# Attention and feed-forward on eight cores: fills spread over whole tiles, square roots split in two steps, and an end worked in subtiles

## The reference

```python
def layernorm(x): return (x - mean(x)) / sqrt(var(x) + 1e-5)
# x: (4, 4096, 1024), 16 heads of 64
q, k, v = heads(ln(x) @ Wq + bq), heads(ln(x) @ Wk + bk), heads(ln(x) @ Wv + bv)
att = q @ k.T / 8
mask = tril(ones(T, T)) * (arange(T) % 4 != 3)      # causal, and every fourth key dropped
att = softmax(where(mask == 0, -inf, att))
x = x + ln((att @ v) @ Wp + bp)
idx = argmax(log_softmax(logits) + gumbel(u))       # one of 8 weight matrices
x = x + ln(ln(x) @ W[idx] + b[idx])
```

## Time and profile before

| | us |
|---|---|
| Median of 3 runs (lowest to highest) | 746.71 (746.45 to 749.49) |
| The profiled execution | 743.47 |
| Its span on the slowest core, core 6 | 741.9 |
| Spans of the eight cores | 733.8 to 741.9 |
| PE, ACT, DVE, POOL busy | 649.0, 530.2, 418.1, 144.0 |

### The profile page before, as it was taken

The page is one execution under the profiler, slowest core; times in us unless marked ns, Lnnn a source line. Parts: engine busy times, 40 slices in busy tenths (PEclk is TensorE's granted clock), DMA queues, the critical chain, the costliest instruction groups (busy, mean ns, idle before and its releaser), DMA issues.

```text
span 741.3 us, 24579 instructions; the slowest of 8 cores (733.8 to 741.9 us)
## 1 busy us (share of the span) xinstructions
PE 649.0 (88%) x9452; PEld 283.8 (38%) x9460; DVE 418.1 (56%) x744; ACT 530.2 (72%) x718; POOL 144.0 (19%) x238
## 2 busy tenths in 40 slices
PE   1788989889898999999999998889999999999846
PEld 1444435344344444333433433333333333333312
DVE  3327766765655463653333333277766776986484
ACT  3233356344698787888878888888898989888246
POOL 1010013122122112212111124110120110760104
PEclk9979999899999999999999999999999999999989
DMA  8989467955357062123400035602233223142224
GB/s 161 185 184 159 147 173 154 208 83 109 99 115 165 18 132 44 32 46 55 93 17 17 18 59 84 190 16 74 83 77 88 75 88 105 34 138 87 102 57 142
DMA packets 78240, 72.47 MB, mean 98 GB/s; under 512 B 58544, under 2 KB 58800, under 8 KB 78128
## 3 DMA queue, kind: packets, MB, share of 16 engines
q1 hardware_dynamic: 72060, 59.50, 31.9%
q0 software_dynamic: 5696, 11.14, 9.6%
q10 hardware_dynamic: 372, 0.27, 0.2%
HBM read 60.68 MB, written 8.52 MB: 93 GB/s over the span
## 4 chain that ended last, share of the span: by engine, by line
PE 50%; ACT 15%; issue 15%; DMA 11%; DVE 6%; SPq 1%; ACTq 1%; POOL 1%; DVEq 0%; POOLq 0%
PE pj L673 23%; ACT Pr L1223 12%; PE sps L744 10%; PE yz L781 7%; PE yz L799 4%; DMA wkb<-wk 3%; DMA wvb<-wv 2%; PE yz L671 2%; DMA fmQ<-tok 1%; PE pj L671 1%; PE sps L847 1%; DVE Vsb L901 1%; DMA zr<-zev 1%; DMA xq<-xkv 1%; DMA xq<-xq 1%
## 5 line engine op out<-in xcount | busy, mean ns | idle before, releaser
L1223 ACT ACTIVATE Pr<-sps,negc 128x1024 bf16<-128x1024 f32 (+1 forms) x416 | 428.8, 1078 | 92.7 <-PE sps L746 90.1
L1354 POOL TENSOR_TENSOR Pr<-Pr,mk_sb 128x172 bf16<-128x172 bf16 x192 | 98.9, 536 | 464.8 <-ACT Pr L1223 464.7
L744 PE MATMUL sps<-QY,Ksb 64*128 64x512 bf16 (+2 forms) x480 | 138.7, 346 | 25.2 <-ACT Pr L1223 23.2
L746 PE MATMUL sps<-QY,Ksb 64*128 64x512 bf16 (+2 forms) x480 | 140.4, 350 | 0.0
L781 PE MATMUL yz<-Pr,Vsb 128*32 128x512 bf16 (+5 forms) x1920 | 125.0, 345 | 5.8 <-POOL Pr L1354 3.2
L744 PEld LDWEIGHTS sps<-QY,Ksb 64*128 64x128 bf16 x480 | 35.8, 93 | 133.5 <-issue 131.2
L799 PE MATMUL yz<-Pr,cbf 128*32 128x512 bf16 (+2 forms) x960 | 82.0, 345 | 0.0
L781 PEld LDWEIGHTS yz<-Pr,Vsb 128*32 128x32 bf16 x1920 | 49.4, 97 | 49.3 <-issue 12.5
L901 DVE TENSOR_TENSOR Vsb<-pj,bvb 128x512 bf16<-128x512 f32 x41 | 28.1, 688 | 52.4 <-PE pj L673 46.7
L673 PE MATMUL pj<-wpb,QY 128*32 128x512 bf16 x768 | 50.7, 381 | 0.1
L673 PE MATMUL pj<-fmQ,wqb 128*32 128x512 bf16 x768 | 48.0, 388 | 2.2 <-DMA fmQ<-tok 2.2
(11 more groups left out here) (195 smaller groups left out, 807.8 us busy)
## 6 DMA issues: line engine op xcount, KB each, us to landing
xin<-xkv SPq DMA_DIRECT2D x21, 512.0 KB, 4.7
xr<-xq SPq DMA_DIRECT2D x16, 512.0 KB, 3.4
zb<-zscr SPq DMA_DIRECT2D x62, 128.0 KB, 3.3
xin<-xq SPq DMA_DIRECT2D x12, 512.0 KB, 4.4
out<-xr SPq DMA_DIRECT2D x12, 512.0 KB, 2.8
wkb<-wk POOLq DMA_DIRECT2D x4, 512.0 KB, 17.8
wvb<-wv POOLq DMA_DIRECT2D x2, 1024.0 KB, 15.8
wqb<-wq POOLq DMA_DIRECT2D x2, 1024.0 KB, 14.2
```

Of the source, the lines that this page charges most:

```text
L744: PE.matmul(sps[s % 2][:, 0, off:off + w], Ksb[0:64, g, hp, kc:kc + 128], QY[0:64, t, hp, n0:n0 + w], start=True, stop=True, tile_position ...
L746: mm = PE.matmul(sps[s % 2][:, 1, off:off + w], Ksb[64:128, g, hp, kc:kc + 128], QY[64:128, t, hp, n0:n0 + w], start=True, stop=True, tile ...
L1223: A.activation(out=Pr[:, s % 4, :, 0:wide], in_=sps[s % 2][:, :, 0:wide], func=AF.Exp, bias=negc[:, k:k + 1], scale=0.125).then_inc(s_exp, 1)
L1354: op = G.tensor_tensor(out=view, in0=view, in1=mk[:, j:j + 1, :].broadcast_to([128, 2, BAND]), op=ALU.mult)
```

## The change

Six things change.

1. `make_order` deals the projection units of a tile over all its pairs and, for tiles 0 and 1, a little into the next (0.2 and 1.0 pairs), where 94% of the pairs were used before. From tile 1 on the first pair of a tile takes none of the new list.
2. The bound C stands after the third V unit of the last group, where it stood last.
3. `pv` waits, in the first head pair of a tile, for the V unit of the chunk that it is about to read, where it waited for the last V unit of the tile.
4. `zroot`, `x1root` and `froot` become two entries each of ACT's queue, planned 1.2 us apart, with what DVE does behind them planned later.
5. For head pair 31 the row sums are made with as many matmuls as values have (`last_rowsum`), so that the sum of a head stands in all 64 rows of that head in `zps`. DVE masks the last two steps (`last_mask`), and for each subtile inverts the sums where they stand and scales (`last_norm`). The DMA steps of head pair 31 are gone.
6. Each of the four last subtiles is closed by `tail_end` right behind its own `tail_begin`, and what the four engines do at the end stands in an order written out by hand.

```diff
@@ proj_units
-    v1 = v1[:2] + [("N", "K", 2 * n + 1, 0)] + v1[2:4] + [("N", "K", 2 * n + 1, 1)] + v1[4:] + [("C", n)]
+    v1 = v1[:1] + [("N", "K", 2 * n + 1, 0)] + v1[1:2] + [("N", "K", 2 * n + 1, 1)] + v1[2:3] + [("C", n)] + v1[3:]
@@ make_order
+    into = [0.2, 1.0, 0.0]
     for t in range(3):
-        fills.update(spread(proj_units(t + 1), BASE[t], COUNT[t] * 0.94))
-    fills.update(spread(post_units(), BASE[3] + 1, COUNT[3] * 0.98))
+        for m, parts in spread(proj_units(t + 1), BASE[t] + (t > 0), COUNT[t] + into[t] - (t > 0)).items():
+            fills.setdefault(m, []).extend(parts)
+    fills.update(spread(post_units(), BASE[3] + 1, COUNT[3] * 0.985))
...
-                act.append((x + 1.2 + 4.0, "zroot", u[1]))
-                dve.append((x + 1.2 + 5.5, "x1", u[1]))
+                act.append((x + 1.2 + 4.0, "zlog", u[1]))
+                act.append((x + 1.2 + 5.2, "zroot", u[1]))
+                dve.append((x + 1.2 + 6.1, "x1", u[1]))
...
+    behind(dve, ("lastmask", 0), ("lastmask", 1), ("fstat", 11), ("lastnorm", 12), ("lastnorm", 13), ("lastnorm", 14),
+           ("tailz", 12), ("lastnorm", 15), ("tailx", 12), ("tailz", 13), ("final", 11), ("tailx", 13), ("tailz", 14),
+           ("tailz", 15), ("tailx", 14), ("tailx", 15), ("tailfs", 12), ("tailfs", 13), ("tailfs", 14), ("tailfs", 15),
+           ("taillast", 15))
@@ pv
-                if hp == 0:
-                    PE.wait_ge(s_evd, EVD_N["V", 2 * t + 1, 2, 1])
...
                 for c, n0, w, off in parts:
+                    if hp == 0:
+                        PE.wait_ge(s_evd, EVD_N["V", c // 3, c % 3, 1])
@@ last_rowsum, new
+            for s in (2 * m, 2 * m + 1):
+                for c, n0, w, off in STEPS[s][1]:
...
+                    for j in (0, 32, 64, 96):
+                        mm = PE.matmul(zps[j:j + 32, n0:n0 + w], cbf[:, 288:320], Pr[:, s % 4, j // 64, off:off + w],
+                                       start=first, stop=final, tile_position=(0, j))
@@ tail_o
             if s == 15:
-                PE.wait_ge(s_ycopy, 32)
-                PE.wait_ge(s_zcopy, 32)
+                PE.wait_ge(s_ynorm, 35)
             tail_begin(s, 0)
-            if s < 15:
-                tail_begin(s, 1)
-            else:
-                PE.wait_ge(s_ynorm, 32)
...
+            tail_begin(s, 1)
+            PE.wait_ge(s_ynorm, s + 20)
+            tail_end(s, 0)
+            tail_end(s, 1)
@@ last_norm, new
+            n0, n1 = 128 * (s - 12), 128 * (s - 11)
+            V.wait_ge(s_pv, NP)
+            V.reciprocal(out=zev[:, 1, n0:n1], in_=zps[:, n0:n1]).then_inc(s_lastinv, 1)
+            V.wait_ge(s_lastinv, s - 11)
+            V.tensor_tensor(out=QY[:, 3, 7, n0:n1], in0=yps[:, n0:n1], in1=zev[:, 1, n0:n1],
+                            op=ALU.mult).then_inc(s_ynorm, 1)
```

More of the change, by code:

```diff
@@ L204, in make_order @@
         ln.update({KV_TILE[2 * t + 4] + i: max(kv_free - 4.0, ln[KV_TILE[2 * t + 4] - 1] + 4.0) + 4.2 * i for i in range(3)})
-        ln.update({KV_TILE[2 * t + 5] + i: start[t + 1] - 2.0 + 5.0 * i for i in range(3)})
+        ln.update({KV_TILE[2 * t + 5] + i: start[t + 1] - 1.0 + 5.0 * i for i in range(3)})
     pe, dve, act, pool, sp = [], [], [], [], []
@@ L295, in make_order @@
             act.append((x, "exp", 2 * m + a))
-            if masked(2 * m + a):
+            if masked(2 * m + a) and m < NP - 1:
                 pool.append((x + 1.1, "mask", 2 * m + a))
-    for k in range(32):
-        x = begin[LAST[k] + 2] if LAST[k] + 2 <= NP else begin[NP] + 1.0
+    for k in range(31):
+        x = begin[LAST[k] + 2]
         dve.append((x, "ycopy", k))
[L301 to L305, removed]
-        again = begin[LAST[k + 2] + 2] - 0.3 if k < 29 else begin[NP] + 20.0
-        dve.append((min(x + 13.5 * late, again), "ynorm", k))
@@ new lines, in make_order, with behind @@
+        dve.append((x + 5.7, "zinv", k))
+        sp.append((x + 6.2, "zout", k))
+        sp.append((x + 10.3, "zback", k))
+        again = begin[LAST[k + 2] + 2] - 0.3 if k < 29 else begin[NP] + 20.0
+        dve.append((min(x + 18.2, again), "ynorm", k))
+    late = max(begin[NP], max(item[0] for item in dve)) + 1.0
+    def behind(queue, *items):
+        queue.extend((late + 0.01 * n, kind, key) for n, (kind, key) in enumerate(items))
+    behind(dve, ("lastmask", 0), ("lastmask", 1), ("fstat", 11), ("lastnorm", 12), ("lastnorm", 13), ("lastnorm", 14),
+           ("tailz", 12), ("lastnorm", 15), ("tailx", 12), ("tailz", 13), ("final", 11), ("tailx", 13), ("tailz", 14),
+           ("tailz", 15), ("tailx", 14), ("tailx", 15), ("tailfs", 12), ("tailfs", 13), ("tailfs", 14), ("tailfs", 15),
+           ("taillast", 15))
@@ L1145, in vector_engine @@
                 final(key)
+            elif kind == "lastmask":
+                last_mask(key)
+            elif kind == "lastnorm":
+                last_norm(key)
             elif kind == "tailz":
@@ L1303, in scalar_engine @@
                 exp(key)
+            elif kind == "zlog":
+                zlog(key)
             elif kind == "zroot":
                 zroot(key)
+            elif kind == "x1log":
+                x1log(key)
             elif kind == "x1root":
                 x1root(key)
+            elif kind == "flog":
+                flog(key)
             elif kind == "froot":
                 froot(key)
[L1310 to L1325 removed]
             elif kind == "tailzroot":
```

107 lines of the change are left out of this document (53 added, 54 removed).

## The result

| | before | after |
|---|---|---|
| Median of 3 runs (lowest to highest), us | 746.71 (746.45 to 749.49) | 756.16 (755.22 to 758.82) |
| Span of the profiled execution, slowest core | 741.9 (core 6) | 754.2 (core 2) |
| Spans of the eight cores | 733.8 to 741.9 | 749.5 to 754.2 |
| PE, ACT, DVE, POOL busy | 649.0, 530.2, 418.1, 144.0 | 656.2, 527.9, 420.8, 142.9 |

The ratio is 1.0129, with a 95% interval of 1.0091 to 1.0168: the change makes the kernel 9.5 us **slower**. Forecast were 736.1 us (729.0 to 743.5), faster with a chance of 0.84. The forecast was wrong in sign.

The account below looks back on a forecast made before the run. PE sets the pace, with ACT close, idle tile ends and a waiting end. Terms -6.3 + 1.5 - 3.0 - 2.8 = -10.6 us give 732.9 profiled; 3.2 for the median gives 736.1, range 729 to 743.5.

Parts of the forecast that it names:

- Fills over whole tiles: Spreading fills into the empty pairs at tile ends recovers PE's idle time there: -3.0 us, from -5.0 to 0.
- the slope of 0.4: Growth of a pair's period per us of fill, taken between no fill and 0.96 us of fill a pair.
- this stays: PE's 1.4 us wait for masks behind a POOL load remains, with two loads (2 x 0.94) ahead of the last mask.
- Rival 4: Tile 0: V evictions on DVE stand behind `zinv` waiting for a DMA; slower, 754.7 us, chance 0.07.
- The end: Closing the last four subtiles one by one removes PE's 8.9 us wait before the feed-forward: 6.3 us less.
- The forecast's own test: Wrong if last row sums to the span's end is not at least 4 us shorter than 50.6.
- Row sums of head pair 31: Four more matmuls in each of 11 pairs cost PE time: +1.5 us, from 1.1 to 2.3.
- Roots: Splitting each root's two ACT steps costs 0.35 instead of 0.52 us, 35 times: -2.8 us, from -5.8 to 0.
- a subtile has some 18 us, which hides it: DVE getting each root one exponential (1.1 us) later costs nothing, given a subtile's some 18 us.
- PE and ACT take turns: The two engines alternate as the limit, so only half of the roots' 5.8 us of ACT was counted.
- The other test: Prediction wrong if the first scores of tile 1 start more than 3 us later than 191.61.

Follow-up runs that it names:

- E2: The kernel before with only the new layout of the fills and the waits for values by chunk: 763.71 us, ratio 1.0192.
- E4: The changed kernel with the output projection's weight loads waiting for unit K(6,2) instead of Q(3,7): 750.78 us, ratio 1.0025.
- E5: The changed kernel with `zinv` of head pair 17 and its following steps planned 8.4 us later, behind two evictions: 750.82 us, ratio 1.0051.
- E6: E4 with loads due between two masks put behind those masks: 747.25 us, ratio 1.0018.
- E14: E6 with norms and bound at their old places among the values, and fills ending with each tile (`into` zero): 743.50 us, ratio 0.9954.
- E10: E6 with `zinv` and its following steps planned 3 us later for head pairs 0 to 6: 747.00 us, ratio 1.0000.
- E3: The kernel before with the new end, row sums of head pair 31 included, and values waited for by chunk: 741.73 us, ratio 0.9926.
- E1: The changed kernel with the fills laid out as before; roots apart and the new end stay: 743.95 us, ratio 0.9946.
- E7: E6 with the fills, norms and bound of tiles 0 and 1 laid out as before: 739.82 us, ratio 0.9925.
- E8: E7 with the two steps of every root together again, planned as before: 741.95 us, ratio 0.9934.
- E9: E7 with `zinv` of head pair 23 and its following steps planned 6 us later: 739.93 us, ratio 0.9896.
- E12: E9 with the two steps of every root together again, planned as before: 741.49 us, ratio 0.9920.
- E15: E7 with the two steps of the z root together for the first three output subtiles: 737.99 us, ratio 0.9881.

## Why the prediction was wrong

**Fills over whole tiles: -3.0 forecast, +14.3 measured (E2).** This step failed. It priced only PE's idle time in the empty pairs, and that time did go. It took zero as the worst case, "by the slope of 0.4", as if a fill could be moved alone. But each fill that moves shifts evictions, loads and masks against their neighbours in four in-order queues, and the range held none of those meetings. Three cost most: K(6,2) behind `zinv` (6.7 us, E4 and E5), masks 223 and 239 behind loads (4.4 us by the traces, E6), and N and C amid single value units, whose earlier place I had put at nothing (2.8 us of PE's waits in tile 0, E14, together with `into`). What tile 1's share consists of stays open. Who would stand behind whom could be read from the queues before any run; how long the waits would be could be guessed at one place, since in the kernel before DVE had waited 4.34 us at this very `zinv`, 8.8 us behind SP's issue. I had even read the loads ahead of the last mask, priced them as two issues of 0.94 and called it "this stays"; but with the time in front of each issue 2.85 us stand between the last two masks, and the wait at pair 120 is 3.3 us and not 1.4.

**Rival 4** had the right kind of mechanism, evictions behind a `zinv` that waits for a DMA, in the wrong place. I looked for it in tile 0, where taking 8 us of these waits away changed no time that E10 could resolve; it struck once, in tile 2, for 9.18 us, above the longest wait of 5.2 that I had taken from the earlier trace rows as a bound. That bound was itself a product of the order before. It named 754.7 us, close to the result, but for the wrong tile and with a chance of 0.07: that the number fits is luck. Its counter-argument (the copies stand further ahead on SP, so the waits get shorter) did not hold for head pair 17: SP sent early, the transfer was late. In tile 0 the waits at `zinv` are 12.5 us as a mean over the cores, 11.3 before.

**The end: -6.3 forecast, -7.4 on the two slowest cores and -6.0 by the medians of eight, -5.5 with its row sums in E3's ratio.** Right, nearly step by step. The inversion took 0.93 to 0.95 us and the cycle 712.57 - 711.33 = 1.24 (1.3 taken); the estimate of 1.2 for the inversion that I had drawn from the Trainium skill (VectorE: DVE Perf Modes, "Walkthrough: the 8-slice pipeline in each mode") was too high, the row-based 0.85 too low. The four scalings took 0.29 us each, 1.16 in all where one took 0.69, the 0.5 more that was forecast. The wait for the transposed inputs, 8.9 us, became 0.5, 2.5 and 0.6; forecast were under 1, then 2 to 3 twice, so the third input came sooner than thought, and the clock did fall behind the wait of 2.5. The forecast's own test (at least 4 us shorter than 50.6 from the last row sums) is met: 754.2 - 710.58 = 43.6.

**Row sums of head pair 31: +1.5 forecast, +1.1 in E3**, +0.7 in the changed kernel's last ten pairs. Right, if at or just under the lower bound of 1.1. (Eleven groups of 0.22 are 2.4 and not 2.3, and 35 times 0.17 for the roots is 6.0 and not 5.8; neither matters.)

**Roots: -2.8 forecast.** The cost per root is even below the 0.35 taken (0.27), and pairs 132 to 189 gain 1.8 to 2.1 us. What failed is "a subtile has some 18 us, which hides it": the first subtiles of tile 3 stand closer, and there 1.1 to 1.9 us come back (E1 against E3, E7 against E8, E9 against E12; E15 regains 1.6 of them). In whole kernels roots apart are worth from +1.5 (E1 against E3) to -2 us (E7 against E8), and the halving for "PE and ACT take turns" was an assumption that no run tests.

**The other test** (first scores of tile 1 more than 3 us later than 191.61) was not met on core 2, which started at 190.02. The median of eight cores was 3.4 later from the start of the attention. A single core's start is a poor test: pairs 0 to 15 scatter between 91.0 and 94.8 us over eleven kernels with the same layout there.

**Sum:** -5.5 (end with row sums) + 14.3 (fills) + 1.5 to -2 (roots) = +7 to +10, measured +9.5. The intervals of the parts, E2's above all, are wider than what this sum leaves over.

## What to carry to other kernels

When work moves, price its new neighbours, not only the gap that it fills: for each engine queue, list what now stands behind a wait for a DMA or behind a DMA issue, and read from the trace how long that wait can get at that very moment. A longest wait of the trace is no bound for another order. Zero is no lower bound for a rearrangement either, where engines work in-order queues: here small repairs of the order and the old layout in two tiles brought back 16 us (E7), more than three times what the rearrangement could have gained.
